# Attention probabilities transposed in 32x32 blocks by VectorE and placed by sixteen on-chip DMAs, with the values product in fp32 one unit later

## What is computed

```python
x = x + L0(x);  x = x + L1(x);  x = x + L2(x)          # 8 sequences of 128 x 512
q = rope(rmsnorm(x @ Wq.T));  k = rope(rmsnorm(x @ Wk.T));  v = x @ Wv.T   # 32 query heads, 8 key heads, D = 128
kc, vc = k_cache[block_table], v_cache[block_table]      # 512 cached positions
k_all, v_all = concat(kc, k), concat(vc, v)               # 640 keys
scores = where(valid, q @ k_all.T * SCALE, -1e30)
probs = softmax(scores)
out = x + (probs @ v_all) @ Wo.T
```

## Time and profile before

| | |
|---|---|
| median of 3 runs | 1242.15 us (1240.19 to 1245.4) |
| the profiled execution | 1239.95 us, of it 1238.1 us between its first and last instruction |
| mean granted TensorE clock | 0.993 of full speed |
| busy: TensorE, VectorE, ScalarE, GpSimd | 98%, 74%, 69%, 44% |
| DMA | 109.50 MB, 88 GB/s over the span |

### The profile page before, as it was taken

How to read it: one execution, slowest core, us unless ns; L and a number is a source line. 1 busy time by engine, 2 the same in 40 slices (tenths; PEclk the granted TensorE clock), 3 DMA queues, 4 the chain that set the end, 5 groups by cost and what they waited for, 6 DMA issues and landing times.

```text
span 1238.1 us, 28992 instructions
## 1 busy us (share of the span) xinstructions
PE 1212.0 (98%) x7072; PEld 1038.2 (84%) x7072; DVE 918.8 (74%) x2295; ACT 853.2 (69%) x2170; POOL 545.5 (44%) x570
## 2 busy tenths in 40 slices
PE   7998999999999999999999999999999999999997
PEld 4565888888888888888888888888888888888885
DVE  2336778777778777787787877877778777777774
ACT  2233777777777777777777777777777777767774
POOL 7761444445444444444444444444544445333430
PEclk9998999999999999999999999999999999999999
DMA  6673222222222222222122222222222222112210
GB/s 193 232 255 107 78 67 78 89 89 67 75 80 89 89 62 80 80 89 89 61 74 87 89 86 65 72 89 89 78 67 77 89 89 69 63 59 85 85 52 25
DMA packets 37607, 109.50 MB, mean 88 GB/s; under 512 B 7512, under 2 KB 7640, under 8 KB 36570
## 3 DMA queue, kind: packets, MB, share of 16 engines
q1 hardware_dynamic: 25288, 68.44, 16.1%
q0 software_dynamic: 11152, 36.72, 10.4%
q10 hardware_dynamic: 1154, 4.19, 0.9%
HBM read 103.03 MB, written 6.29 MB: 88 GB/s over the span
## 4 chain that ended last, share of the span: by engine, by line
PE 96%; DVE 1%; ACT 1%; DMA 1%; issue 1%; POOL 0%; SPq 0%; DVEq 0%; ACTq 0%; POOLq 0%
PE ps_q L794 14%; PE ps_ring L858 12%; PE ps_o L694 11%; PE ps_o L696 11%; PE ps_o L695 11%; PE ps_kv L794 7%; PE ps_s L696 6%; PE ps_s L694 6%; PE ps_s L695 6%; PE ps_l L726 2%; PE ps_ring L820 2%; PE ps_q L828 2%; PE ps_t L688 1%; PE ps_l L742 1%; PE ps_h L712 1%
## 5 line engine op out<-in xcount | busy, mean ns | idle before, releaser
L622 ACT ACTIVATE prob<-prob,low 128x640 f32<-128x640 f32 x256 | 210.8, 824 | 129.0 <-DVE low L1112 128.9
L1028 DVE TENSOR_TENSOR pt_lo<-ps_ring,pt_hi 128x512 fp32r<-128x512 f32 x320 | 209.1, 686 | 87.8 <-ACT pt_hi L582 87.5
L1112 DVE CUSTOM_DVE_ANT_0 prob<-ps_s,mask,q_gain 128x640 f32<-128x640 f32 x256 | 216.3, 882 | 36.8 <-PE ps_s L696 35.0
L103 POOL TENSOR_TENSOR w_lo<-w_raw,w_hi 128x640 f32 (+1 forms) x64 | 100.2, 1565 | 263.6 <-DVE w_hi L97 262.3
L582 ACT ACTIVATE pt_hi<-ps_ring 128x512 fp32r<-128x512 f32 x320 | 181.5, 593 | 33.1 <-PE ps_ring L858 33.0
L627 ACT ACTIVATE prob<-prob,inv 128x640 f32<-128x640 f32 x256 | 196.9, 818 | 0.0
L858 PE MATMUL ps_ring<-ident,prob 128*128 128x128 f32 x1280 | 186.3, 276 | 5.1 <-DVE pt_lo L1028 2.7
L858 PEld LDWEIGHTS ps_ring<-ident,prob 128*128 128x128 f32 x1280 | 149.0, 141 | 40.3 <-DVE pt_lo L1028 9.9
L794 PE MATMUL ps_q<-w_hi,x_s 128*128 (+1 forms) x512 | 171.8, 396 | 0.0
L694 PE MATMUL ps_s<-kt_hi,qt_hi 128*128 (+1 forms) x512 | 159.4, 311 | 1.5 <-DVE low L1112 1.5
L696 PE MATMUL ps_s<-kt_hi,qt_lo 128*128 (+1 forms) x512 | 159.5, 311 | 0.0
(11 more groups left out here) (141 smaller groups left out, 2587.8 us busy)
## 6 DMA issues: line engine op xcount, KB each, us to landing
x_s<-xt_split SPq DMA_DIRECT2D x64, 512.0 KB, 3.3
w_raw<-w_qkvo_dram SPq DMA_DIRECT2D x55, 320.0 KB, 3.5
w<-w_t_dram SPq DMA_DIRECT2D x8, 1024.0 KB, 6.8
xt_split<-x3t ACTq DMA_DIRECT2D x8, 512.0 KB, 4.3
w_raw<-w_qkvo_dram POOLq DMA_DIRECT2D x9, 320.0 KB, 4.9
xbt<-x_t_dram SPq DMA_DIRECT2D x8, 256.0 KB, 2.9
xb<-x_dram SPq DMA_DIRECT2D x8, 256.0 KB, 3.7
out_dram<-y SPq DMA_DIRECT2D x8, 256.0 KB, 2.2
```

The costliest lines, as they stand in the source:

```text
L103: return nc.gpsimd.tensor_tensor(lo, raw, hi.bitcast(F32), ALU.subtract)
L622: nc.scalar.activation(prob[:, h, :], prob[:, h, :], ACT.Exp, bias=low[:, h:h + 1], scale=-1.0, accum_out=total[:, h:h + 1]).then_inc(exp_ ...
L1028: return nc.vector.tensor_tensor(dst, src, high.bitcast(F32), ALU.subtract)
L1112: nc.vector.tensor_tensor_reduce(out=prob[:, h, :], in0=ps_s[:, score_slot(h):score_slot(h) + KEYS], in1=mask[:, :], scale=q_gain[:, h:h + ...
```

## The change

1. `turn_probs`, `chunk_high` and `chunk_low` go. For each head, when it is normalized, VectorE transposes `prob` in 32x32 blocks (`turn_blocks`, one instruction of 128x640) into `blocks`. When all four heads are done, SyncE issues sixteen DMAs from SBUF to SBUF, each 32 partitions x 640 elements of 4 bytes (82 KB, 1.31 MB a unit), which put block row and block column where a full transpose has them, in `prob_t` (`place_blocks`).
2. The values product takes `v_raw` and `prob_t` as plain fp32: 2 pairs of heads x 5 chunks, 256 columns wide. The split of the values (`values_high`, the low part on GpSimd and of the new value on VectorE) goes. The new value is copied by ScalarE to `v_next` and by GpSimd to `v_new`.
3. `values(n-1)` runs in TensorE's step n, between the second pair of scores and the turn of the rotated queries; `put_out(n-1)` follows it. The output is converted in two halves (`out_high`, `out_low`, 128x256 each), and the addition to y comes one unit later. `turn_cached` handles unit n+1 in place of n+2; the projections of queries and of key and value run as one block behind the first pair of scores.
4. On SyncE the input is loaded one unit later in the loop's count: step n waits for `kv_proj` >= n+2, loads the input of unit n+2, then the weight piece n+9, and then places the blocks of unit n.
5. The semaphore waits that go with it: `turn_blocks(n, 0)` waits until the sixteen DMAs of unit n-1 have landed, `place_blocks(n)` for the four transpositions of the unit and for the values product n-2, `values(n-1)` for the DMAs of n-1.

```diff
@@ SyncE
-                    def step(n, weights, last, finished):
-                        if not last:
-                            sp.wait_ge(kv_proj, n + 1)
-                            sp.dma_start(x_s ...)
+                    def next_input(u):
+                        sp.wait_ge(kv_proj, u)
+                        sp.nop(nofuse=True)
+                        sp.dma_start(x_s[:, :, :].bitcast(F32), xt_dram[bass.ds(u & 7, 1), :, :, :] ...).then_inc(x_s_in, 16)
+
+                    def place_blocks(n, first=False):
+                        sp.wait_ge(blocks_turned, GROUP * (n + 1))
+                        sp.nop(nofuse=True)
+                        if not first:
+                            sp.wait_ge(pv_done, 2 * n)
+                        sp.nop(nofuse=True)
+                        for a in range(NB):
+                            for j in range(NB):
+                                sp.dma_start(prob_t[j * BLOCK:(j + 1) * BLOCK, a, :, :, :] ...,
+                                             blocks[a * BLOCK:(a + 1) * BLOCK, j, :, :, :] ...).then_inc(pt_in[j], 16)
+
+                    def step(n, inputs, weights, finished, first=False):
+                        if inputs:
+                            next_input(n + 2)
                         if weights:
                             sp.wait_ge(w_split, n + AHEAD)
                             sp.dma_start(w_raw[:, 0, :], w_qkvo[bass.ds(n + AHEAD, 1), :, :] ...).then_inc(w_raw_in, 16)
+                        place_blocks(n, first)
+                        if finished:
+                            store_out(n - 2)
@@ TensorE
+                    def values(u, first=False):
+                        pe.wait_ge(v_in, 16 * (u + 1))
+                        pe.wait_ge(vn_moved, u + 1)
+                        for j in range(NB):
+                            pe.wait_ge(pt_in[j], 16 * NB * (u + 1))
+                        if not first:
+                            pe.wait_ge(ot_lo_out, 2 * u)
+                        for pair in (0, 1):
+                            for c in range(CH):
+                                v = v_raw[:, c * D:(c + 1) * D] if c < CCH else v_new[:, :]
+                                mm = nc.tensor.matmul(ps_o[pair][:, 0:PAIR], v,
+                                                      prob_t[:, :, c, 2 * pair:2 * pair + 2, :] ...,
+                                                      start=c == 0, stop=c == CH - 1)
+                            mm.then_inc(pv_done, 1)
@@ TensorE, step
                         score_pair(n, 0)
                         if not last:
                             project_queries(n + 1)
+                            project_new_key(n + 1)
+                            turn_cached(n + 1, n - 1 if wait_added else None)
                         score_pair(n, 1)
+                        if not first:
+                            values(n - 1, first=second)
                         if not last:
                             turn_rotated(n + 1)
+                        if not first:
+                            pe.wait_ge(kc_lo_out, n + 1 if last else n + 2)
+                            put_out(n - 1)
@@ VectorE
+                    def turn_blocks(n, h, first=False):
+                        dve.wait_ge(prob_done, GROUP * n + h + 1)
+                        if h == 0 and not first:
+                            for j in range(NB):
+                                dve.wait_ge(pt_in[j], 16 * NB * n)
+                        nc.vector.transpose(blocks[:, :, :, h, :] ..., prob[:, h, :] ...).then_inc(blocks_turned, 1)
@@ VectorE, step
+                        if add:
+                            add_out(n - 2)
                         if weights:
                             weights_high(n)
                         lowest(n, 0)
                         lowest(n, 1)
                         inverse(n, 0)
-                        values_high(n, first)
                         inverse(n, 1)
+                        if not last:
+                            rotate_queries(n + 1)
+                            rotate_queries_rest(n + 1)
+                        turn_blocks(n, 0, first)
+                        turn_blocks(n, 1)
+                        if not last:
+                            variances(n + 1)
+                            rotate_key(n + 1)
                         lowest(n, 2)
                         lowest(n, 3)
                         if not last:
                             cached_low(n + 1)
+                        if not first:
+                            out_low(n - 1, 0)
                         inverse(n, 2)
                         inverse(n, 3)
+                        if not first:
+                            out_low(n - 1, 1)
+                        turn_blocks(n, 2)
                         if not last:
                             rotated_low(n + 1)
                             gains(n + 1)
+                        turn_blocks(n, 3)
@@ ScalarE, step
-                    def step(n, keys, last, first=False):
+                    def step(n, last, first=False, second=False):
                         exps(n, 0)
                         exps(n, 1)
                         normalize(n, 0)
                         normalize(n, 1)
+                        if not last:
+                            query_squares(n + 1, range(GROUP))
+                            key_squares(n + 1)
+                            new_value(n + 1, first=first)
+                            cached_high(n + 1, first=first)
                         exps(n, 2)
+                        if not first:
+                            out_high(n - 1, 0, first=second)
                         exps(n, 3)
                         if not last:
                             scale_key(n + 1)
                         normalize(n, 2)
+                        if not first:
+                            out_high(n - 1, 1, first=second)
                         if not last:
                             rotated_high(n + 1)
                         normalize(n, 3)
```

More of the change, by code:

```diff
@@ L32 @@
 AHEAD = B + 1
+BLOCK = 32
+NB = P // BLOCK
 THETA = 10000.0
@@ L356, in _ @@
+                    store_out(UNITS - 1)
                     sp.wait_ge(out_in, 16 * B)
@@ L466, in norm_factors, with move_new_value, step @@
                         nc.gpsimd.tensor_tensor(rstd[:, :], var[:, :], neg_half[:, :], ALU.pow).then_inc(rstd_done, 1)
-                    def step(n, weights, keys, last):
-                        vl = v_lo[:, 0:CCH, :].rearrange("p c d -> p (c d)")
-                        vh = v_hi[:, 0:CCH, :].rearrange("p c d -> p (c d)")
+                    def move_new_value(u, values):
+                        pool.wait_ge(vn_out, u + 1)
+                        if values:
+                            pool.wait_ge(pv_done, 2 * u)
+                        pool.nop(nofuse=True)
+                        nc.gpsimd.tensor_copy(v_new[:, :], next_value(u)).then_inc(vn_moved, 1)
+                    def step(n, weights, keys, values, last):
                         if weights:
@@ L483, in step @@
                             norm_factors(n + 1)
+                        if keys:
+                            next_keys(n + 2)
+                        move_new_value(n, values)
+                        if values:
+                            next_values(n)
                     sum_queries(0, first=True)
@@ L669, in _ @@
                     key_squares(0)
+                    new_value(0, first=True)
                     second_low_rank(B - 1)
@@ L675, in _ @@
                     store(B - 1)
-                    step(0, True, False, first=True)
-                    with act.Fori(1, UNITS - 2) as n:
-                        step(n, True, False)
-                    step(UNITS - 2, False, False)
-                    step(UNITS - 1, False, True)
-                    out_high(UNITS - 1)
+                    step(0, False, first=True)
+                    step(1, False, second=True)
+                    with act.Fori(2, UNITS - 1) as n:
+                        step(n, False)
+                    step(UNITS - 1, True)
+                    out_high(UNITS - 1, 0)
+                    out_high(UNITS - 1, 1)
                 @block.tensor
@@ L870, in step @@
-                    def step(n, keys, last, first=False):
-                        if first:
-                            pe.wait_ge(kc_lo_out, 1)
-                            turn_cached(1)
+                    def step(n, last, first=False, second=False, wait_added=True):
                         pe.wait_ge(qt_lo_out, n + 1)
@@ L930, in _ @@
                     turn(ps_t3, x3, t3_done)
-                    step(0, True, False, first=True)
-                    with pe.Fori(1, UNITS - 2) as n:
-                        step(n, True, False)
-                    step(UNITS - 2, False, False)
-                    step(UNITS - 1, False, True)
+                    step(0, False, first=True, wait_added=False)
```

(10 more changed lines are left out.)

218 lines of the change are left out of this document (73 added, 145 removed).

## The result

The changed kernel takes **1999.45 us** (median of 4 runs, 1995.35 to 2003.56); the kernel before took 1243.78 us beside it. The ratio is 1.608 [1.602, 1.614]. The forecast was 1745 us with a range of 1580 to 1910: the direction is right, the size lies 254 us too low.

What follows compares the result with a forecast made beforehand. TensorE bound the kernel before; the change puts a late weight piece behind sixteen placing issues, a 26.1 us loop. 1240 + 484 (55 units x 8.8) + 16 (8 x 2.0) + 5 (last unit) = 1745 us, range 1580 to 1910.

Steps and rivals of the forecast that it cites:

- Point 1: SyncE's sixteen placing issues, one after another, at 0.45 us each (ends 0.32 and 0.70): 7.2 us of the loop.
- Points 2 and 3: From the input's issue to the weight piece's, 0.7 us; then landing of the piece, 3.5 us (ends 2.2 and 4.9).
- Points 4 to 9: VectorE's and ScalarE's path from rounding the landed piece to the last transposition: 0.5, 4.1, 1.7, 0.9, 4.3 and 3.0 us.
- Point 6: Four squares of queries, 1.1 us, then square of the key and copy of the new value, 0.6: 1.7 us.
- point 9: VectorE's end of the unit: half of the output's low part, transposition, low parts and gains, last transposition: 3.0 us together.
- Units without a piece: From unit 55 on, the loop runs through the landing of the placed blocks: 19.3 us, 2.0 above before.
- The clock: TensorE drops to 1.2 GHz after idling, slowing scores and values by about 2.5 us; 0.2 us reaches the loop.
- Issues are cheap: Rival: the data sets the placing's pace, 4.0 us in place of 7.2; about 1543 us; chance 6%.
- The transpositions are slow: Rival: VectorE's transpositions take 1.57 us each; 1905 us; chance 5%.
- the piece isn't late: Rival: VectorE's wait for the weight piece is covered, all units take 19.3 us; 1366 us; chance 3%.
- the clock stays low: Rival: TensorE at 1.2 GHz throughout, 31.6 us a unit in place of 15.8; at least 2141 us; chance 3%.
- TensorE stays the bound at 1145 us: Rival: TensorE's 15.8 us a unit sets the time, with the piece in time and placing short; chance 2%.

Runs made afterwards that it cites:

- s1: Changed kernel with the weight piece loaded by SyncE a round earlier, sixteen placing issues kept: 1545.46 us.
- x4: Changed kernel, weight piece still late, one placing DMA of 128 rows in place of sixteen (output not the reference's): 1685.64 us.
- s3: Changed kernel with the weight piece a round earlier and one placing DMA in place of sixteen (output not the reference's): 1151.23 us.
- x5: Changed kernel with the sixteen placing DMAs reading weights in DRAM instead of the turned blocks on the chip: 1824.65 us.
- x1: Changed kernel with each of the sixteen placing DMAs carrying 64 of its 640 columns: 1993.31 us.
- x3: Changed kernel with sixteen placing DMAs of 16 rows x 640 columns, half of the data: 2000.03 us.

## Why the prediction was right in kind and wrong in size

The terms below are counted against the profiled execution, 1995.35 us, which is 250 above the forecast.

- **Which loop sets the time: right.** The late weight piece (454 us by `s1`) behind the placing (314 us by `x4`) is the loop; with both gone TensorE is the bound again (`s3`). Each alone leaves the other, so together they are worth 848 us, more than the sum of 768.
- **Point 1, sixteen issues at 0.45 us: this is the step that failed.** The issues stand 0.63 us apart, and up to the input's issue it is 10.70 us where 7.2 stood. That is 3.5 us in each of 55 units, 192 of the 250 us missed. By `x5` it has two parts. 2.73 us are the dear source, 150 us in all. The other 0.77, 42 us, remain with issues at 0.46: they are mostly the 0.68 us from the end of the last issue to the input's issue (937.38 to 938.06), for which the sum had no term. The price was read from the earlier trace rows, and for DMAs that read DRAM it was good: `x5` shows 0.46. A row of a DMA between two places on the chip was not in the profile of before, and I carried the price over to it; neither bytes nor rows count (`x1` to `x3`), the source does (`x5`). My upper end of 0.70 held the measured value, but within the range it was given only the weight of 0.36 to 0.55. The text had set its own bound: wrong if the issues are over 0.6 apart.
- **Points 2 and 3**: 0.66 for 0.7. The landing was right, its median is the 3.5 us predicted; but VectorE starts 3.93 us after the issue, and the 0.4 in between had no term: 24 us.
- **Points 4 to 9: right in sum, 14.50 us for 14.5, with some luck.** Point 6 is 0.4 too short and point 9 0.2 too long, which nearly cancels. From the timeline: `lowest` 0.40 after the rounding's start (0.5); to the end of the second `normalize` 4.10 (4.1); squares and new value 2.08 (1.7), ScalarE waiting 0.4 for VectorE's rotation; variances and key 0.92 (0.9); up to the last `ot_lo` 4.24 (4.3); the end 2.76 (3.0). A transposition is 0.83 us long and 0.76 from the next, not the 0.88 of `lowest`. The prediction's estimate of 0.84, worked out from the 311 ns that the Trainium skill has on the page "VectorE: DVE Perf Modes", section "The three transpose paths", agrees with the trace.
- **Units without a piece**: 21.7 us (placing issues at 1947.08 and 1968.71; 1816.76 seven units before that), 19.3 predicted. Placing to values is 11.7 us for 9.4; the rest is as predicted. 8 x 2.4 = 19 us. The remaining 15 us lie outside the 63 distances from one unit's placing to the next, at the start and the end, where I had put 5.
- **The clock: right, and it cost the loop nearly nothing.** The windows of the changed kernel (us, PE, PEld, DVE, ACT, POOL, granted clock, DMA share, GB/s):

```profile
900.00:902.00 2.00, 2.00 (x12) 1.69 (x11) 0.00 (x0) 0.00 (x0) 0.00 (x0) 1.00 0.58 137
904.00:906.00 2.00, 0.00 (x0) 0.00 (x0) 0.00 (x0) 0.00 (x0) 0.00 (x0) 1.00 0.52 123
908.00:910.00 2.00, 0.00 (x0) 0.00 (x0) 0.00 (x0) 0.00 (x0) 0.00 (x0) 0.50 0.66 182
...
918.00:920.00 2.00, 2.00 (x7) 1.64 (x6) 1.67 (x7) 1.62 (x10) 1.42 (x2) 0.50 0.00 0
920.00:922.00 2.00, 2.00 (x11) 1.77 (x10) 2.00 (x6) 0.92 (x3) 1.21 (x3) 0.98 0.00 0
```

  TensorE stands idle from 903.4 to 914.8, and its scores and the first values run at 1.2 GHz up to 920. That is why it is busy for 1275.8 us here and for 1116.3 in `s3`, 2.5 us a unit for the same instructions, as the prediction had it. The cover held: this work is not last. The 0.2 us that I had taken for the clock are not in the loop; that SyncE begins 0.21 us after the last transposition, which had no term, takes their place by luck.
- **The signs.** TensorE is busy for 64% of the span (about 60%), VectorE waits 14.6 us for the piece (9 to 11), TensorE 11.2 for the row lows (7 to 8), and a unit without a piece takes 21.7 us (19). The two waits and the unit are off mainly by the issues. The wait for the piece is not the longest of all, as the text had it, but the third, behind two that follow from it.
- **The rivals.** "Issues are cheap" fell with the issue rows. The sentence of the Trainium skill that it was given with, page "DMA: Bandwidth & Descriptors", section "Issuing engines are not separate DMA queues", says that the sequencer's time to initiate a DMA is usually small relative to the DMA itself. For a single DMA here it is smaller, 0.59 us against 2.1 from issue to landing. But the issues of one queue add up and the landings overlap, so that sixteen issues occupy SyncE for 10.0 us and only one landing stands behind them. "The transpositions are slow" fell at 0.83 us, "the piece isn't late" and "the clock stays low" with the rows above. "TensorE stays the bound at 1145 us" is what `s3` shows at 1151: its mechanism was right, and its two conditions, the piece in time and the placing short, are just those that the changed kernel doesn't meet.

## What to carry to other kernels

In this kernel a DMA costs its issuing engine 0.3 to 0.6 us, and in the bursts the price didn't depend on what it carried: count the issues, price them with a row of the same source and destination, and see what stands behind them, loads of the next round above all. Work taken from the bound engine is worth nothing while a load that used to be a round early becomes part of the loop; ask for it ahead of the burst. When the issues can't be fewer, give them to queues in which nothing urgent follows. With the piece asked for early, the shares 16 on one queue, 8 and 8, and 9, 2 and 5 gave 24% and 10% slower than before and 1.5% faster, the last with the transpositions moved as well.

## What the runs showed of the hardware that was not expected

- An issue that reads and writes on the chip takes 0.59 us on SyncE and 0.63 to the next in a burst, with 64 to 640 columns and 16 to 128 rows; one that reads DRAM takes 0.42 and 0.46 in the same burst; a single one of 128 rows between two places on the chip takes 0.49, and single ones from DRAM 0.33.
- On ScalarE's queue an issue is 0.60 to 0.64 us long, on GpSimd's 0.52, so GpSimd was not the dearest of the three. The landing was longer when several queues issue at once: 2.1 us with one, 2.3 to 2.4 with 10 and 6 on two, 2.7 with 8 and 8, 2.6 to 3.0 with 9, 2 and 5 on three, and 3.3 to 3.7 with 8, 4 and 4.
